# Expert stage of a two-part transformer block: the scaled input is split into f16 halves in SBUF and transposed by DMA, instead of transposed on TensorE and split out of PSUM

## What is computed

```python
rw = _gating(hidden_states, sim_matrix, gates)          # [b, t, 16]
q = jnp.einsum('bte,bted->btd', rw, jnp.einsum('btc,ecd->bted', hidden_states, q_proj))
k = jnp.einsum('bte,bted->btd', rw, jnp.einsum('btc,ecd->bted', hidden_states, k_proj))
v = jnp.einsum('bte,bted->btd', rw, jnp.einsum('btc,ecd->bted', hidden_states, v_proj))
scores = jnp.einsum('bqd,bkd->bqk', q, k) * scale
scores = jnp.where(causal, scores, -jnp.inf)
attn = jnp.einsum('bqk,bkd->bqd', jax.nn.softmax(scores, axis=-1), v)
mixed = attn[:, :, None, :] * rw[..., None]
return jnp.einsum('bted,edc->btc', mixed, o_proj)
```

## Time and profile before

| | |
|---|---|
| three runs | 1552.88, 1553.21, 1555.73 us (median 1553.21) |
| the profiled execution | 1555.85 us |
| its span in the trace | 1554.1 us, granted clock 0.973 of full speed |
| PE busy | 1314.9 us (85%) |
| DVE busy | 1280.1 us (82%) |
| POOL busy | 1107.2 us (71%) |
| ACT busy | 1049.4 us (68%) |

### The profile page before, as it was taken

The page is one execution under the profiler, slowest core; times in us unless marked ns, Lnnn a source line. Parts: engine busy times, 40 slices in busy tenths (PEclk is TensorE's granted clock), DMA queues, the critical chain, the costliest instruction groups (busy, mean ns, idle before and its releaser), DMA issues. The chain is left out here.

```text
span 1554.1 us, 27938 instructions
## 1 busy us (share of the span) xinstructions
PE 1314.9 (85%) x8882; PEld 803.2 (52%) x8882; DVE 1280.1 (82%) x2129; ACT 1049.4 (68%) x1967; POOL 1107.2 (71%) x715
## 2 busy tenths in 40 slices
PE   2888888888888888888888888888853899999997
PEld 1444444444444444444444444444432899899997
DVE  5899999899999999998999999998866566656665
ACT  2887777777777777777777777787633455445553
POOL 3898888888888888888888888888834333323330
PEclk8899999999999999999999999999975999999999
DMA  4221111111111112111111211110030000000000
GB/s 110 72 74 46 46 28 50 42 52 31 46 46 27 46 37 57 34 46 46 27 46 34 57 37 46 28 28 1 1 54 1 5 6 8 8 8 7 8 9 10
DMA packets 51461, 52.99 MB, mean 34 GB/s; under 512 B 17057, under 2 KB 32929, under 8 KB 51361
## 3 DMA queue, kind: packets, MB, share of 16 engines
q1 hardware_dynamic: 51360, 51.76, 13.2%
HBM read 7.68 MB, written 2.10 MB: 6 GB/s over the span
## 5 line engine op out<-in xcount | busy, mean ns | idle before, releaser
L1214 DVE TENSOR_REDUCE negmax<-score_ps 128x1 f32<-128x1024 f32 x512 | 618.8, 1216 | 87.9 <-PE score_ps L569 86.0
L904 ACT ACTIVATE prob<-score_ps,negmax 128x1024 f32<-128x1024 f32 x512 | 571.5, 1116 | 129.4 <-DVE negmax L1214 117.7
L465 POOL TENSOR_TENSOR prob<-prob 128x1024 f32<-128x1024 f32 x256 | 604.2, 2360 | 21.3
L569 PE MATMUL score_ps<-ka,qa 128*128 128x512 f16 x1024 | 313.0, 388 | 119.4 <-ACT prob L904 105.9
L463 POOL TENSOR_SCALAR prob<-prob,ccol 128x1024 f32<-128x1024 f32 x256 | 287.2, 1122 | 104.7 <-DVE ccol L1227 104.2
L592 PE MATMUL trans_ps<-ident,prob 128*128 128x128 f32 x2048 | 283.9, 277 | 7.4 <-POOL prob L465 3.0
L592 PEld LDWEIGHTS trans_ps<-ident,prob 128*128 128x128 f32 x2048 | 240.3, 142 | 75.8 <-DVE probT L318 17.7
L598 PE MATMUL attn_ps<-probT,v_sb 128*64 128x512 f32 x1024 | 276.7, 620 | 1.1 <-DVE probT L318 1.1
L517 POOL TENSOR_TENSOR xs<-xnT,rw_all 128x2048 f32 (+1 forms) x32 | 115.5, 3612 | 210.9 <-PE t_ps L722 204.1
L569 PEld LDWEIGHTS score_ps<-ka,qa 128*128 128x128 f16 x1024 | 72.4, 98 | 277.5 <-ACT prob L904 233.4
L318 DVE COPY probT<-trans_ps 128x512 f32<-128x512 f32 x256 | 174.0, 680 | 2.4 <-PE trans_ps L592 2.4
(11 more groups left out here) (195 smaller groups left out, 1423.6 us busy)
## 6 DMA issues: line engine op xcount, KB each, us to landing
qa<-split SPq DMA_DIRECT2D x256, 64.0 KB, 2.0
ka<-split SPq DMA_DIRECT2D x256, 64.0 KB, 2.0
xg<-xnT SPq DMA_DIRECT2D x16, 512.0 KB, 3.0
resid<-in_L_attn_x SPq DMA_DIRECT2D x4, 512.0 KB, 6.0
wg<-in_L_attn_Wkv SPq DMA_DIRECT2D x32, 64.0 KB, 1.9
out<-yo SPq DMA_DIRECT2D x32, 64.0 KB, 1.5
wg<-in_L_attn_Wq SPq DMA_DIRECT2D x16, 64.0 KB, 1.9
ew<-in_L_ffn_q_proj SPq DMA_DIRECT2D x1, 512.0 KB, 4.5
```

The lines of the kernel that those rows point to most:

```text
L465: pool.tensor_tensor(prob1[:, u, :], prob1[:, u, :], prob2[:, u, :], ALU.add).then_inc(mix_ok, 1)
L569: mm = pe.matmul(score_ps[:, sub, kh * HALF:(kh + 1) * HALF], qa[:, par, head * 2 + sub, q0:q0 + P], ka[:, par, head * 2 + sub, kh * HALF: ...
L904: act.activation(prob2[:, s % 4, :] if sub else prob1[:, s % 4, :], score_ps[:, sub, :], ACT.Exp, bias=negmax[:, s % 2, sub:sub + 1], accu ...
L1214: dve.tensor_reduce(negmax[:, s % 2, sub:sub + 1], score_ps[:, sub, :], AX.X, ALU.max, negate=True).then_inc(max_ok, 1)
```

## The change

`x_transposes` and the four `x_copy` of ACT and of DVE go. In their place ACT writes the high half of the whole tile from `xs` to `xs_split` in SBUF (`x_high`, one operation of 2048 elements a partition), DVE writes the low half from `xs` and the high half (`x_low`, again 2048 elements), and SP issues one DMA transpose for each half (`transpose_x`, 512 KB each), which writes `xsT`. `xsT` is four tiles deep instead of two, and the split of tile m + 2 is done in the round of tile m, at its start. `x_high` of tile m + 2 waits until both DMA transposes of tile m have landed, as they share the `xs_split` buffer. POOL's operation for tile m waits until the low half of tile m - 1 is written. SP's program is written out, and the store of tile m - 6 stands behind the transposes of tile m. To make room, `p2`, `mx` and `xs_split` now lie in `prob2` and `prob1`, the first part's buffers, so the profile and the order name them `prob`.

```diff
+X_AHEAD = 2
+X_BUFS = 4
...
-        xsT = sb("xsT", [P, 2, 2, E, P], F16)
+        xsT = sb("xsT", [P, X_BUFS, 2, E, P], F16)
...
+            def transpose_x(tile):
+                r, buf = tile % 2, tile % X_BUFS
+                if tile >= X_BUFS:
+                    sp.wait_ge(qkv_ok, tile - X_BUFS + 1)
+                for part, ready in enumerate((xs_hi, xs_lo)):
+                    sp.wait_ge(ready, tile + 1)
+                    sp.dma_start_transpose(xsT[:, buf, part, :, :],
+                                           xs_split[:, r, part, :, :].rearrange("p e c -> p (e c)")).then_inc(xT_in[buf], 16)
...
+            for tile in range(B * NT + X_AHEAD + PART2_LAG):
+                if tile < B * NT:
+                    transpose_x(tile)
+                if tile >= X_AHEAD + PART2_LAG:
+                    store(tile - X_AHEAD - PART2_LAG)
...
             def scale_by_experts(m, r, peeled):
                 if not peeled:
-                    pool.wait_ge(xT_ps, 4 * (m - 1))
+                    pool.wait_ge(xs_lo, m)
...
+            def x_high(m, r):
+                act.wait_ge(xs_ok, m + 1)
+                act.activation(xs_split[:, r, 0, :, :], xs[:, r, :, :], ACT.Copy).then_inc(xs_hi, 1)
...
+                    if not (last and t + X_AHEAD >= NT):
+                        act.wait_ge(xT_in[t % X_BUFS], 32 * (NT // X_BUFS * it + t // X_BUFS + 1))
+                        x_high(m + X_AHEAD, t % 2)
...
+            def x_low(m, r):
+                dve.wait_ge(xs_hi, m + 1)
+                dve.tensor_tensor(xs_split[:, r, 1, :, :], xs[:, r, :, :], xs_split[:, r, 0, :, :],
+                                  ALU.subtract).then_inc(xs_lo, 1)
```

More of the change, by code:

```diff
@@ L180, in block_kernel @@
         x2sq = prob1
+        xs_split = prob1[:, :, :].bitcast(F16).rearrange("p (r n) (e c) -> p r n e c", r=2, c=C)
         x2n = xnT.rearrange("p (t c) -> p t c", c=C)
@@ L235, in block_kernel @@
         qkT = sb("qkT", [P, 3, T], F16)
-        p2 = sb("p2", [P, 2, T])
+        p2 = prob2[:, 2:4, :]
         p2T = sb("p2T", [P, NT, P])
@@ L240, in block_kernel @@
         rec2 = sb("rec2", [P, 2])
-        mx = sb("mx", [P, 2, E, DE])
+        mx = prob2[:, 0:2, :].rearrange("p r (e d) -> p r e d", d=DE)
         mxT = sb("mxT", [P, 2, E // 2, P], F16)
@@ L277, in block_kernel @@
                                     "normed_V", "T", "A", "V", "lg", "v", "exp", "rw"))
-        (xs_ok, xT_ps, xT_hi, xT_lo, qkv_ok, hi2, lo2, kv_read, kv_first_ok, qkt_ps, qkt_ok, s2_ok, max2, exp2, pT_ps,
+        xT_in = [sem(f"p2_xT_in{n}") for n in range(X_BUFS)]
+        (xs_ok, xs_hi, xs_lo, qkv_ok, hi2, lo2, kv_read, kv_first_ok, qkt_ps, qkt_ok, s2_ok, max2, exp2, pT_ps,
          pT_A, pT_V, pv2, rec2_ok, mx_ok, mT_ps, mT_hi, mT_lo, y_ok, y_done) = (sem("p2_" + n) for n in (
-            "xs", "xT_ps", "xT_hi", "xT_lo", "qkv", "hi", "lo", "kv_read", "kv_first", "qkt_ps", "qkt", "s", "max", "exp",
+            "xs", "xs_hi", "xs_lo", "qkv", "hi", "lo", "kv_read", "kv_first", "qkt_ps", "qkt", "s", "max", "exp",
             "pT_ps", "pT_A", "pT_V", "pv", "rec", "mx", "mT_ps", "mT_hi", "mT_lo", "y", "y_done"))
@@ L405, in _, with store @@
                              eo.rearrange("(g two) d c -> two d g c", two=2)[half]).then_inc(experts_in, 16)
-            def store(tile, r):
-                sp.wait_ge(y_done, tile + 1)
[L409 to L413, removed]
+            def transpose_x(tile):
[6 more added lines that the diff above has]
+                                           xs_split[:, r, part, :, :].rearrange("p e c -> p (e c)")).then_inc(xT_in[buf], 16)
+            def store(tile):
+                sp.wait_ge(y_done, tile + 1)
+                sp.dma_start(out_rows[:, tile:tile + 1, :], yo[:, tile % 2:tile % 2 + 1, :]).then_inc(stored[tile % 2], 16)
+            for tile in range(B * NT + X_AHEAD + PART2_LAG):
[3 more added lines that the diff above has]
+                    store(tile - X_AHEAD - PART2_LAG)
             for r in range(2):
@@ L521, in _ @@
             scale_by_experts(0, 0, True)
-            scale_by_experts(1, 1, True)
+            scale_by_experts(1, 1, False)
             with pool.Fori(1, B * NT // 2) as pair:
@@ L703, in bank_read @@
                         for what in before:
[L704 to L709, removed]
                             if what == "p" and live(2):
@@ L713, in bank_read, with experts @@
                                 return pe.wait_ge(mT_lo, 2 * (m - 4) + bank + 1)
-                    def x_transposes(group, bank):
+                    def experts(group):
                         if not live(0):
@@ L718, in x_transposes @@
                         if group == 0:
[L719 to L729, removed]
+                            pe.wait_ge(xT_in[t % X_BUFS], 32 * (NT // X_BUFS * it + t // X_BUFS + 1))
                         if group == 0 and not (first and t == 0):
@@ L735, in experts @@
                             for n, (x_part, w_part) in enumerate(SPLIT_PRODUCTS):
-                                mm = pe.matmul(qkv_ps[:, 0:3 * DE], xsT[:, t % 2, x_part, e, :], ew_split[:, w_part, e, :],
+                                mm = pe.matmul(qkv_ps[:, 0:3 * DE], xsT[:, t % X_BUFS, x_part, e, :], ew_split[:, w_part, e, :],
                                                start=e == 0 and n == 0, stop=e == E - 1 and n == 2)
@@ L748, in p_transposes @@
                             return
-                        bank_read(bank, ("x0", "y of m - 1"))
+                        bank_read(bank, ("y of m - 1",))
                         for kb in range(4 * bank, min(v, 4 * bank + 3) + 1):
@@ L760, in m_transposes @@
                             pe.wait_ge(mx_ok, m - 2)
-                        bank_read(bank, ("x1", "p", "y of m - 1"))
+                        bank_read(bank, ("p", "y of m - 1"))
                         for g in range(4):
@@ L805, in tiles2 @@
                     experts(1)
-                    x_transposes(2, 0)
-                    x_transposes(3, 1)
                     if live(2):
@@ L973, in _ @@
             act.activation(gl[:, 8, :, :], gl[:, 7, :, :], ACT.Exp).then_inc(g_exp, 1)
+            def x_high(m, r):
+                act.wait_ge(xs_ok, m + 1)
+                act.activation(xs_split[:, r, 0, :, :], xs[:, r, :, :], ACT.Copy).then_inc(xs_hi, 1)
+            for m in range(X_AHEAD):
+                x_high(m, m % 2)
             def tiles2(it, first, last):
@@ L1355, in _ @@
             link(dve.tensor_tensor(rw_all[:, :, :], gl[:, 9, :, :], per_token(gs[:, 1, :]), ALU.mult), rw_ok)
+            def x_low(m, r):
+                dve.wait_ge(xs_hi, m + 1)
+                dve.tensor_tensor(xs_split[:, r, 1, :, :], xs[:, r, :, :], xs_split[:, r, 0, :, :],
+                                  ALU.subtract).then_inc(xs_lo, 1)
+            for m in range(X_AHEAD):
+                x_low(m, m % 2)
             def tiles2(it, first, last):
@@ L1362, in live @@
                         return not (first and t < lag) and not (last and t - lag >= NT)
[L1364 to L1373, removed]
+                    if not (last and t + X_AHEAD >= NT):
+                        x_low(m + X_AHEAD, t % 2)
                     if live(4):
```

6 lines of the change are left out of this document (removed).

## The result

The changed kernel takes 1519.04 us (median of 4 runs, 1518.89 to 1519.63) against 1553.28 us before (median of 4 runs): the ratio is 0.9777, interval 0.976 to 0.9794, or 34 us less. The forecast was 1527. The profiled execution of after took 1519.09 us, with a span of 1517.3 us.

The account below looks back on a forecast made before the run. PE's program was taken to bound the stage after 1189 us, then a ring of ACT, DVE and PE. Spacings -40 and start +14 gave -26 us: 1530 from the profiled 1555.85, 1527 as median; range 1505 to 1680.

Parts of the forecast that it names:

- The bound and what goes: Stage after 1189 us: PE's program sets the pace; dropping 512 transposes lowers its floor from 10.59 to 8.83 us a tile.
- `x_high` and `x_low`: New split operations of 2048 elements: 1.9 us on ACT for the high half, 2.3 us on DVE for the low half.
- The ring: Steady rounds: a chain through ACT, DVE and PE sets 9.25 us a tile, so 1.34 of 1.76 us remain, -40 us.
- PE's main wait for DVE `mxT`: Sign that the forecast is right: PE waits mainly for DVE's `mxT`, with `qs` spacings near 9.3 us.
- The start: First tiles of the stage: POOL, ACT and DVE go hand in hand, +12 us, plus 2 for PE's clock, +14.
- The loop's turn: Turn of PE's hardware loop: the 3.2 us gap and its cold stretch, clock 0.72 over 12 us, stay.
- The transposes: DMA transposes of each tile's two halves: 2.3 to 3.0 us each, hidden within a 9.25 us round, costing nothing.
- Block by block at issue: Rival: each of a half's 16 blocks costs an issue of 0.40 us, 6.4 us a half; 1637 us, chance 0.27.
- Latency by latency: Rival: blocks transpose one after another, each paying its whole latency, 48 us a tile; 2728 us, chance 0.12.
- `x_low` beside POOL: Rival: DVE's `x_low` meets POOL's `xs` and takes 5.2 us, ring 12.15 us a tile; 1614 us, chance 0.07.

## Why the prediction was right, point by point

**The bound and what goes.** Right in the main: PE's floor was the bound. I put the new floor at 8.83 us; the kernel with almost no split shows 8.5 to 8.6. What I had wrong is a reading: "PE itself waits for next to nothing in the steady part". It waited 9.0 us for the low halves that DVE wrote, in the same stretch as the earlier trace rows:

```profile
PE t_ps L764 <- DVE xsT L1368: 6.4, 13, 0.8
PE qkv_ps L736 <- DVE xsT L1368: 2.6, 5, 1.0
```

These waits went with the transposes. A batch without the loop's turn took 84.46 us before (1372.97 to 1457.43 us), of which PE was busy 82.79, that is 10.35 a tile. Less 1.76 this is 8.59.

**`x_high` and `x_low`.** 1.9 and 2.3 us forecast, 1.92 and 2.29 measured. Twice the solo row of 1024 elements less one fixed part was the right reading.

**The ring.** 1.34 us saved a tile forecast, 1.46 measured over 29 spacings. The chain of ACT and DVE ends above PE's floor, as said, and PE waits for `mxT`. But in the steady part that is the smaller wait, 3.2 us from 1240 to 1440 us. The larger one, 5.0 us, was not named: in the heavy tiles DVE's `p2T` copy stands behind `x_low` and holds PE ahead of `o_ps`, up to 1.0 us. With the copy on ACT, eight spacings take 70.3 us, 8.8 each, against 72.8 and 9.1 in the same batch of the changed kernel. So what I had as the ring, 9.25 us, was too long by some 0.4, and the size came out near through a wait that I had not named. That is in part luck, and "PE's main wait for DVE `mxT`" is true of the stage as a whole (9.5 us), not of its steady part. I counted the copy in the chain of DVE, with 0.25 us, but did not ask who waits for it. Moving it to ACT gained 6.7 us by the traces.

**The start.** +14 forecast, +13.5 measured, in the steps that were written down: hand in hand through POOL, ACT and DVE, and ACT's `x_high` of tile 2 ahead of tile 0's copies. The 2 us that I had put down for the clock are there as well: PE's granted clock was 0.71 from 1204 to 1220 us, against 1.00 at that place before, and tile 1's 48 expert products took 6.6 us (2.12 and 4.43) against 4.4 (1.15, 1.15 and 2.14) in a later tile.

**The loop's turn.** This step failed: "The gap at the loop turn and its cold stretch (clock 0.72 over 12 us) stay." They went, worth 6.6 us by the medians of the kernel with the loop written out and 6.0 to 6.2 by the spacings. It is most of the difference between 26 forecast and 34 measured; the other 29 spacings gave 3.5 us more than forecast. I had called it a gap with no releaser and left it; the number of instructions of a body is an effect of the change that I didn't count.

**The transposes.** Hidden, as taken, with a half at "2.3 to 3.0 us". The size was off: a half lands after 4.5 us, and costs 3.1 to 3.2 us of the DMA engines, 169 GB/s (524,288 bytes in 3.1 us) instead of the row's 230. Two of them take 6.3 us of a round of 9.1: they are hidden with a margin of a third, not of a half. The 261 GB/s of the Trainium skill, "DMA: Bandwidth & Descriptors", section Latency and other measured facts, is above what is measured here; the 1309 ns for one block of the Trainium skill, "VectorE: DVE Perf Modes", section The three transpose paths, is no rate here, since 16 blocks land in 4.5 us, 0.28 us each.

**The rivals.** Block by block at issue: each block would have had to cost 0.40 us of SP; SP is held 2.1 us by 16, 0.13 each. That rival had the right resource and three times its price, and I gave it too much. Latency by latency, 24 us a half: excluded. `x_low` beside POOL: it didn't happen in the changed kernel, where `x_low` took 2.29 us. The one that comes later waits, and the price is the rest of the other's instruction: `x_low` took up to 3.68 us where POOL was well under way. My bound took the row beside POOL as a rate and doubled it; it was a wait, which doesn't grow with the length of the operation that waits. The row itself fits that the earlier trace rows: POOL's first operation of 1024 elements began at 1140.71 us, and with 1.8 us for it (half of 3.61, an estimate) DVE had 1.4 us to wait and then 1.23 to work, 2.6 in all.

## What to carry to other kernels

Work that leaves the engine which sets the pace is worth its own time only down to the next ring: write the new order of the in-order engines down and follow one round through it, with each wait of the pacing engine asked for by name. Where one side of a pair of engines has time to spare, let it be the one that comes second at a shared resource, and don't order the two with a wait that also ties the start. And count the instructions of a hardware loop's body before and after: a turn that costs a fetch and a cold clock is worth more than its gap looks.

## What the runs showed of the hardware

A DMA transpose of 128 x 2048 f16 from SBUF to SBUF: SP held about 2.1 us, 4.5 us from issue to landing, 3.1 us of the 16 DMA engines. At the DMA share of 0.7 that this made, PE did not wait for it.

DVE with two SBUF inputs and POOL's `xs` excluded each other for a whole instruction: POOL went from 3.61 to 5.52 us when DVE was first, DVE from 2.29 to 3.65 us when POOL was.

A semaphore increment of its own behind matmuls, 40 in a row, cost PE about 0.12 us.

PE's loop body of 1,567 instructions is not fetched again in the second round, bodies of 1,864 and 1,887 are. Before, the turn then cost a gap of 3.2 us and, with the clock at its lower level of 1.2 GHz behind it, 6.0 to 6.6 us in all. The same program written out was fetched too and had no gap.
